# The last attention in the twelfth step instead of the eleventh, and the last job's layer norm at the end of its step

## What is computed

```python
x = x + 0.5 * ffn(layernorm(x))      # "first"
x = x + attention(layernorm(x))      # "att"
x = x + 0.5 * ffn(layernorm(x))      # "second"
```

## Time and profile before

| | us |
|---|---|
| median of three runs | 152.18 |
| the runs | 152.72, 152.18, 150.43 |
| the profiled execution's own time | 150.15 |
| its span | 148.3 |
| TensorE busy in the span | 142.2 (96%) |
| ScalarE, VectorE, GpSimd busy | 128.5, 126.3, 96.5 |

### The profile page before, as it was taken

The page is one execution under the profiler, slowest core; times in us unless marked ns, Lnnn a source line. Parts: engine busy times, 40 slices in busy tenths (PEclk is TensorE's granted clock), DMA queues, the critical chain, the costliest instruction groups (busy, mean ns, idle before and its releaser), DMA issues.

```text
span 148.3 us, 3010 instructions
## 1 busy us (share of the span) xinstructions
PE 142.2 (96%) x945; PEld 126.5 (85%) x945; DVE 126.3 (85%) x437; ACT 128.5 (87%) x255; POOL 96.5 (65%) x142
## 2 busy tenths in 40 slices
PE   7899999999999999999999999999899999999990
PEld 7699898889889889988988989888789898979790
DVE  3994478689699999999989999999999999464674
ACT  3376979899999998979999999799798997978861
POOL 1448134968899928993999899979953954450200
PEclk9999999999999999999999999999999999999999
DMA  4975000000000000000000001000020011120222
GB/s 139 260 201 162 7 0 0 0 0 7 0 0 0 4 4 0 0 0 0 4 0 2 0 20 55 2 0 0 0 73 4 26 44 39 37 71 0 71 71 71
DMA packets 10510, 5.09 MB, mean 34 GB/s; under 512 B 1152, under 2 KB 10496, under 8 KB 10496
## 3 DMA queue, kind: packets, MB, share of 16 engines
q1 hardware_dynamic: 9808, 4.53, 10.6%
q10 hardware_dynamic: 688, 0.39, 0.9%
HBM read 2.82 MB, written 2.10 MB: 33 GB/s over the span
## 4 chain that ended last, share of the span: by engine, by line
PE 68%; DVE 14%; ACT 8%; issue 4%; DMA 3%; POOL 2%; ACTq 1%; DVEq 0%
PE work L1003 28%; PE hidden L924 8%; PE hidden L928 8%; PE hidden L925 7%; PE work L937 3%; DMA proj_raw<-in_L_ffn_W_proj_dram 3%; ACT signs L520 2%; PE att_work L1034 2%; PE att_value L1058 2%; DVE stats_att L602 2%; ACT square L497 2%; PE att_work L924 2%; PE att_work L928 2%; PE att_work L925 2%; DVE weight_sum L766 2%
## 5 line engine op out<-in xcount | busy, mean ns | idle before, releaser
L1003 PE MATMUL work<-proj_t,square 128*128 128x128 f32 x480 | 61.7, 276 | 0.1
L1003 PEld LDWEIGHTS work<-proj_t,square 128*128 128x128 f32 x480 | 59.0, 192 | 2.9 <-POOL square L425 0.5
L520 ACT ACTIVATE signs<-work 128x512 uint8<-128x512 f32 x73 | 41.3, 620 | 5.3 <-PE work L1003 5.3
L492 ACT ACTIVATE relu<-hidden 128x512 f32<-128x512 f32 x64 | 38.0, 626 | 0.0
L497 ACT ACTIVATE square<-relu 128x512 f32<-128x512 f32 x53 | 35.5, 670 | 0.3
L924 PE MATMUL hidden<-in_hi,fc_lo 128*128 128x512 f32 (+1 forms) x66 | 27.5, 417 | 0.1
L928 PE MATMUL hidden<-in_lo,fc_hi 128*128 128x512 f32 (+1 forms) x66 | 25.7, 389 | 0.0
L925 PE MATMUL hidden<-in_hi,fc_hi 128*128 128x512 f32 (+1 forms) x66 | 25.4, 385 | 0.0
L404 POOL TENSOR_TENSOR rstd<-var_eps,minus_half 128x4 f32<-128x4 f32 x15 | 15.3, 1021 | 14.6 <-DVE neg_mean L615 14.6
L410 POOL TENSOR_SCALAR normed_att<-x_att,neg_mean_att,rstd_att 128x128 f32<-128x128 f32 x32 | 18.3, 581 | 0.8
L675 DVE TENSOR_TENSOR in_lo<-work,in_hi 128x512 fp32r<-128x512 f32 x15 | 10.2, 678 | 9.1 <-ACT in_hi L488 9.0
(11 more groups left out here) (117 smaller groups left out, 251.7 us busy)
## 6 DMA issues: line engine op xcount, KB each, us to landing
x_first<-_attn_hidden_states_dram SPq DMA_DIRECT2D x7, 256.0 KB, 4.2
out_dram<-x_out SPq DMA_DIRECT2D x7, 256.0 KB, 2.2
out_dram<-x_out SPq DMA_DIRECT2D x4, 64.0 KB, 1.5
x_first<-_attn_hidden_states_dram ACTq DMA_DIRECT2D x1, 128.0 KB, 2.7
x_first<-_attn_hidden_states_dram SPq DMA_DIRECT2D x1, 128.0 KB, 2.4
fc_raw<-in_L_ffn_W_fc_dram SPq DMA_DIRECT2D x1, 128.0 KB, 2.7
fc_raw<-in_L_ffn_W_fc_dram ACTq DMA_DIRECT2D x1, 128.0 KB, 3.0
proj_raw<-in_L_ffn_W_proj_dram SPq DMA_DIRECT2D x1, 128.0 KB, 3.6
```

The costliest lines, as they stand in the source:

```text
L492: nc.scalar.activation(relu[j.lane][:, c, :], bank_of_hidden(j, c)[:], ACT.Relu).then_inc(relu_made[j.lane], 1)
L520: nc.scalar.activation(signs[j.lane][:, k, :], work[j.lane][:], func, bias=bias, scale=scale).then_inc(signs_made[j.lane], 1)
L1003: last = nc.tensor.matmul(work[j.lane][:, tokens], square[j.lane][:, c, tokens], proj_t[:, c, :], start=(c == 0 and t == 0), stop=(c == NC ...
```

## The change

The last attention (batch 7) moves from step 11 to step 12. Its values so move to step 13, and its pooling, product, turn back and add to step 14. Since the add of batch 7 now comes in step 14, the layer norm of job 15 can't stand at the beginning of step 14 on VectorE any more. It is moved to the end of that step, and on GpSimd its normalisation moves from loop 13 to the end of loop 14, behind the square of job 14. Job 11 now has its chunk 0 squared by VectorE and job 12 has all four squared by ScalarE.

```diff
--- before.py
+++ after.py
@@ -41,7 +41,7 @@
           [("second", 0)] + \
           [("first", 7)] + \
           [("second", b) for b in range(1, 8)]
-ATT_STEP = [3, 4, 5, 7, 8, 9, 10, 11]
+ATT_STEP = [3, 4, 5, 7, 8, 9, 10, 12]
 CONTRACT_ORDER = (0, 1, 2, 3)
 
 DVE_SQUARES = [(0,), ()]
@@ -455,7 +455,8 @@
 
             for i in range(FIRST_STEP, STEPS):
                 for j in feed_forward(i + 2):
-                    ff_normalise(j)
+                    if not j.is_last:
+                        ff_normalise(j)
                 for b in attention(i + 2):
                     att_normalise(b)
                 for b in attention(i + 1):
@@ -463,6 +464,9 @@
                     att_guess_share(b)
                 for j in feed_forward(i):
                     ff_squares(j)
+                for j in feed_forward(i + 1):
+                    if j.is_last:
+                        ff_normalise(j)
 
 
         @block.scalar
@@ -862,12 +866,12 @@
                         first_normalise(j, 1)
                         first_half_lo(j)
                         other_fc_low_parts()
-                    else:
+                    elif not j.is_last:
                         ff_layer_stats(j)
                 for j in feed_forward(i - 2):
                     ff_sum_sign(j, 3)
                 for j in feed_forward(i + 1):
-                    if j.index > 0:
+                    if j.index > 0 and not j.is_last:
                         ff_layer_args(j)
                 for b in attention(i - 1):
                     att_weight_key(b)
@@ -909,6 +913,10 @@
                         ff_dve_square(j, 2)
                 for b in attention(i):
                     att_sum(b)
+                for j in feed_forward(i + 1):
+                    if j.is_last:
+                        ff_layer_stats(j)
+                        ff_layer_args(j)
                 if i == 0:
                     attention_weights()
                 if i == 1:
```

## The result

The changed kernel takes 156.43 us (median of four runs, 154.82 to 157.86) against 151.5 us before (four runs, 150.43 to 152.72). The ratio is 1.030, with a 95% interval of 1.024 to 1.036: slower by some 4.6 us. (It is taken from the quicker executions of each kernel, 154.82 and 155.7 us for the changed one, and so is smaller than the ratio of the medians.) The forecast was 1.7%, 2.65 us, with a change of less than 2% as the likelier outcome (0.57). The time lies in the forecast range, but that is luck in part: it is there by way of the first rival, which had a chance of 0.12, and of a gain that did not come.

The account below looks back on a forecast made before the run. TensorE, busy 142.2 of 148.3 us, was taken as the bound; step 14 opening 1.02 us earlier and an 11.40 us chain gave 150.15 + 2.65 = 152.8 us profiled, 154.8 us against the median (1.7% slower), range 152.0 to 157.0.

Parts of the forecast that it names:

- Rival 1: TensorE's clock falls in the standstill before job 15's transpositions, making later matmuls slow: +4.35, 156.5 us; chance 0.12.
- a gain that did not come: Step 11's wait for weight_key goes, so step 14 opens 1.02 us earlier.
- The chain of the late layer norm: In step 14, square to last transposition of job 15 ends 11.40 us after the opening; TensorE's own work ends at 7.63.
- The opening of step 14: Steps 11, 12, 13 take 7.93, 9.1, 7.66 us, so step 14 opens at 126.95, 1.02 us earlier than 127.97.
- Nothing else is late in its place: Around step 11: weight_key of batch 6 gets a whole step, so its wait goes without another lateness replacing it.
- the fourth square of ScalarE in step 12: Job 12's square handed from VectorE to ScalarE, claimed to cost nothing on the path.
- What follows ... with the waits that it has now: Behind job 15's transpositions: about 9 us of TensorE's own work to the last contraction, waits as now.
- Rival 2: GpSimd normalises job 14 late too, TensorE waits 0.6 to 0.8 us: +3.4, 155.6 us; chance 0.12.
- Rivals 3 and 4: Relief outweighs late layer norm, 151.1 us, 0.7% faster; or nothing moves, the add being on no path; together chance 0.05.
- The sum: Whole kernel: 150.15 + 2.65 = 152.8 us profiled, 154.8 us against the median, 1.7% slower.
- The upper bounds of the parts: Step 14's opening +1.0 and tiles +0.8 among the parts; whole change put at +2.0 to +4.0 us.
- The chances of "slower": Chance 0.41 of over 2% slower, from the forecast's 0.19 with the two rivals and the stalls.

Follow-up runs that it names:

- experiment 1: Changed kernel with the last attention back in step 11 and the old squares, only job 15's layer norm late; ratio to the kernel before 1.028.
- experiment 4: Changed kernel, but in step 14 VectorE does batch 7's add and job 15's layer norm before job 14's squares; ratio to the kernel before 1.019.
- experiment 7: Changed kernel with job 15's four tiles normalised on VectorE behind GpSimd's power, not on GpSimd; ratio to the kernel before 1.025.
- experiment 6: Changed kernel with the squares of jobs 11 and 12 where they were in the kernel before; ratio to the kernel before 1.031.
- Experiment 2: Changed kernel with filler matmuls on ones before the last transpositions and behind each of the first three tiles; ratio to the kernel before 1.023.
- experiment 3: Changed kernel, but TensorE contracts chunks 2 and 3 of job 14 before it transposes job 15; ratio to the kernel before 1.021.
- experiment 5: Experiment 4's kernel, with chunk 2 of job 14 contracted ahead of job 15's transpositions; ratio to the kernel before 1.010.
- experiment 9: Kernel before, with VectorE's weight_key of the attention before moved ahead of the next job's layer norm statistics; ratio to the kernel before 1.014.

## Why the prediction was right or wrong

- **The chain of the late layer norm: right.** Each of its stations came within 0.15 us of the forecast: `neg_mean` 8.07 against 8.18, tiles 11.00 against 11.10, contraction 11.32 against 11.40. Experiments 1, 4 and 7 shift it as its links say.
- **The opening of step 14, "1.02 us earlier": wrong,** this term of the sum measured 0.02. The wait of step 11 went, as forecast. Step 12 took 9.20 (9.1). But step 11 took 8.27 instead of 7.93 and step 13 8.22 instead of 7.66. "Nothing else is late in its place" was the mistake. Step 12 of the kernel before was no fair template for step 11: VectorE had no statistics of a following attention in it. In the changed kernel they stand in front of the add for which the values product waits (it ends at 111.46, the product starts at 111.51). That is 0.15 us of the 0.34. Another 0.16 is in the contraction at 104.47 (2.11 us for 16 matmuls instead of 1.95); by the rows it waits for ScalarE's square of its last chunk, which ends 1.34 us behind the opening instead of 1.08, but no run tested that. And the fourth square of ScalarE in step 12, which I costed at nothing, holds up the contraction of job 12's last chunk at the start of step 13, as the row of its weight load shows; experiment 6 takes that away, and 0.36 us with it.

```profile
123.06 0.97 PEld L1011 LDWEIGHTS work<-proj_t,square 128*128 128x128 f32 x8 [0.24 <-ACT square L501]
```

- **"What follows ... with the waits that it has now": wrong,** it took 2.35 us more in the profiled execution, and nearly all of that was the clock (some 0.1 lies behind the expansions, where the clock is up again). The same stretch took 9.26 us in experiment 7, 9.79 in 1 and 10.47 in 6, against 8.19 at full clock: 1.1 to 2.3 us more. Rival 1 had the mechanism and about the price (1.7 us, from the slow matmuls at the start); its chance was far too low. My argument against it, that the standstill was short and no row shows a fall, was no argument: a trace without any standstill can't show what one does. Experiment 2 shows that it is the lack of work on TensorE. In 1, 3 and 4 it fell in some executions and not in others of the same kernel; those in which it fell took 1.8, 0.7 and 1.2 us more. What decides it there, no run tells.
- **Rival 2** didn't take place: job 14's transpositions didn't wait. GpSimd ended their tiles at 126.21 + 2.63 = 128.84, 0.9 us ahead. **Rivals 3 and 4** are out by the result itself, and experiment 1 shows the price of the late layer norm alone.
- **The sum:** the forecast 2.65 us had 3.7 of standstill, -1.0 of gain in front of it and no clock in it. The standstill was right (3.6), the gain was nothing, and the clock cost 1.1 to 2.35. An estimate for the quicker executions, with a granted clock of 0.985 as experiment 7 had, takes the lower price: 3.6 + 1.1 = 4.7 against the measured 4.6.
- **Slips in the working:** 138.35 - 135.68 is 2.67, and the sum took 2.65. The upper bounds of the parts add up to +4.45, not +4.0, and none of them was for the clock. The chances of "slower" add up to as much as 0.46, not 0.41. None of it decides anything.

The Trainium skill (TensorE: Matmul & The Clock Gate, "The HAM clock gate") describes an array that is gated to half rate when it has been idle. The trace agrees: granted clock 0.50, and in the changed kernel the fall comes in the standstill, 0.2 us before the first transposition. The same page ("PE-mode transpose") says that transpositions do not count as activity in the way that matmuls do. No run here tests that by itself; in experiments 1 and 4 the clock fell while TensorE did its transpositions.

## What to carry to other kernels

Work that is moved out of a full engine into the tail of a pipeline needs cover there: count the slack of its input (4.5 us here) against the whole distance of the move (a step, 7.3), before looking at what the old place gains. When a change makes TensorE stand idle for some microseconds, cost the matmuls behind the gap at half the clock too, even if the trace at hand has a flat clock row. Useful contractions put into the gap shorten it, and can keep the clock up as well (experiments 3 and 5). A step of the trace is a template for another only if all engines have the same neighbours in it, not just TensorE.

## What the runs showed that I had not expected

- The clock can fall without any long idle time. In experiment 4 the two longest gaps ahead of the fall are 0.61 and 0.35 us, with eight matmuls between them and transpositions behind, and the 16 matmuls that followed took 3.43 us.
- VectorE's short 16-bit adds are held up by GpSimd's products: 1.23 us instead of 0.28 in experiment 9, and in the changed kernel too, in step 13. There, as the rows read (no run moved this one), it makes VectorE late for the square on which TensorE then waits 0.2 us. Timelines of VectorE and GpSimd of the changed kernel:

```profile
124.13 1.10 DVE L756 TENSOR_TENSOR sign_sum<-sign_sum,signs 128x256 uint16<-128x256 uint16 x1
125.19 0.70 DVE L784 SCALAR_TENSOR_TENSOR share_bank<-share_bank,guess_share 128x512 f32<-128x512 f32 x1
```

```profile
123.80 1.28 POOL L453 TENSOR_TENSOR guess_share<-weight_key,guess 128x512 f32<-128x512 f32 x1
```

  It looks the same in the earlier trace rows: VectorE's square took 1.15 us, having started 0.44 us behind GpSimd's square (132.26, 1.04 us); in experiment 4 VectorE's square starts first, takes 0.68, and GpSimd's power beside it is the one that takes longer, 1.38 for 1.01. The Trainium skill (SBUF — State Buffer, "Who interferes with whom") says that a VectorE instruction with two SBUF inputs and a GpSimd instruction that reads SBUF exclude each other, and that whichever comes second waits until the first is through. The trace agrees: the add ends 0.15 us behind the product.
- At the start of the kernel the granted clock reads 1.00, but the matmuls there take 0.24 us each, much as those at a granted clock of 0.50 do (3.62 us for 16, 0.23 each). Either the clock row is wrong there or something else makes them slow; no run tells which.
